# A selective-state scan on one core: projection tiles from a unit's first step, and D times xs by GpSimd in place of a weight product

## What is computed

```python
xz = h @ in_w
xs, z = jnp.split(xz, 2, axis=-1)          # 512 channels each
xs = jax.nn.silu(xs)
proj = xs @ xproj_w
dt = jax.nn.softplus(proj[..., :512] + dt_bias)
Bm, Cm = proj[..., 512:576], proj[..., 576:]   # 64 states
A = -jnp.exp(A_log)
def step(hst, ins):
    dt_t, B_t, C_t, x_t = ins
    dA = jnp.exp(dt_t[:, :, None] * A)
    hst = hst * dA + (dt_t * x_t)[:, :, None] * B_t[:, None, :]
    y_t = jnp.einsum('bds,bs->bd', hst, C_t)
    return (hst, y_t)
_, ys = jax.lax.scan(step, h0, (tm(dt), tm(Bm), tm(Cm), tm(xs)))
y = jnp.swapaxes(ys, 0, 1) + xs * Dskip
return y * jax.nn.silu(z) @ out_w
```

## The kernel before

| tile | what | pieces |
|---|---|---|
| xs (u+1), zs (u) | input projection, 4 tiles each | 2, each a 128x512 product of two passes (L1429) |
| bc (u+1) | B and C | 4 |
| dt (u+1) | dt, 4 tiles | 4 |
| out (u-1) | output projection, 2 tiles | 4 |
| yT (u-1), bT, dtxT (u+1) | four transposes (L1523, L1502, L1512) | 1 |

## Time and profile before

### The profile page before, as it was taken

One profiled execution on the slowest core, in us unless ns is written; L12 is line 12 of the kernel. 1 busy time (PEld: TensorE's weight loads), 2 busy tenths in 40 slices (PEclk: granted clock), 3 DMA queues, 4 the chain that ended last, 5 costly groups with the idle time before them and its releaser, 6 DMA issues.

```text
span 3270.9 us, 59384 instructions
## 1 busy us (share of the span) xinstructions
PE 3194.7 (98%) x22634; PEld 2505.6 (77%) x22634; DVE 2866.5 (88%) x2863; ACT 2815.5 (86%) x4659; POOL 2327.7 (71%) x1113
## 2 busy tenths in 40 slices
PE   8999999999999999999999999999999999999899
PEld 5888898999899998999998999999888542222244
DVE  3999999999999999999999999999999578888121
ACT  6999999999999999999999999999989436777620
POOL 1899999999999999999999999999878220000000
PEclk8999999999999999999999999999999999999999
DMA  3223222212222222222222222222212043422000
GB/s 121 69 84 81 80 72 69 72 67 72 69 73 93 70 70 75 72 69 72 73 73 74 67 72 67 74 68 71 86 57 69 29 102 59 77 34 31 15 7 20
DMA packets 199837, 218.82 MB, mean 67 GB/s; under 512 B 79969, under 2 KB 149601, under 8 KB 199297
## 3 DMA queue, kind: packets, MB, share of 16 engines
q1 hardware_dynamic: 199554, 215.02, 23.1%
HBM read 194.29 MB, written 18.19 MB: 65 GB/s over the span
## 4 chain that ended last, share of the span: by engine, by line
PE 76%; ACT 15%; DVE 6%; issue 3%; DMA 0%; POOL 0%; DVEq 0%; ACTq 0%; SPq 0%
PE psum L1661 21%; PE psum L1429 17%; PE psum L1655 16%; PE psum L1652 12%; ACT arena L1091 6%; ACT arena L1073 5%; PE psum L1739 4%; PE psum L1728 3%; DVE arena L1319 2%; PE psum L1712 2%; DVE row_max L1382 2%; PE psum L1681 1%; ACT arena L1116 1%; ACT arena L1076 0%; ACT arena L920 0%
## 5 line engine op out<-in xcount | busy, mean ns | idle before, releaser
L1319 DVE TENSOR_TENSOR_SCAN arena<-arena,psum 128x512 f32<-128x512 f32 x2048 | 2373.8, 1230 | 58.6 <-PE psum L1655 45.6
L789 POOL TENSOR_TENSOR arena<-arena 128x1024 f32<-128x1024 f32 x1024 | 2225.8, 2185 | 257.1 <-DVE arena L1319 233.5
L1091 ACT ACTIVATE arena<-arena,a_neg 128x512 f32<-128x512 f32 x2048 | 1442.9, 724 | 45.4 <-PE psum L1655 44.9
L1661 PE MATMUL psum<-ident,arena 128*128 128x128 f32 x8192 | 1231.9, 273 | 1.7 <-POOL arena L789 1.7
L1073 ACT ACTIVATE arena<-arena,bT 128x512 f32<-128x512 f32 x1536 | 1110.7, 723 | 0.0
L1655 PE MATMUL psum<-ident,arena 128*128 128x128 f32 x6144 | 1009.8, 273 | 0.0
L1661 PEld LDWEIGHTS psum<-ident,arena 128*128 128x128 f32 x8192 | 962.7, 141 | 2.1 <-POOL arena L789 2.1
L1652 PE MATMUL psum<-arena 128*128 128x128 f32 x4096 | 821.1, 282 | 31.8 <-ACT arena L1073 16.5
L1652 PEld LDWEIGHTS psum<-arena 128*128 128x128 f32 x4096 | 648.3, 191 | 246.6 <-issue 151.9
L1655 PEld LDWEIGHTS psum<-ident,arena 128*128 128x128 f32 x6144 | 744.2, 142 | 0.0
L1429 PE MATMUL psum<-arena 128*128 128x512 f32 (+1 forms) x1440 | 672.0, 587 | 5.2 <-DVE arena L1191 2.9
(11 more groups left out here) (118 smaller groups left out, 871.9 us busy)
## 6 DMA issues: line engine op xcount, KB each, us to landing
arena<-bc_dram SPq DMA_DIRECT2D x256, 512.0 KB, 3.7
arena<-diag_dram SPq DMA_DIRECT2D x224, 128.0 KB, 2.1
arena<-qk_dram SPq DMA_DIRECT2D x96, 128.0 KB
diag_dram<-arena SPq DMA_DIRECT2D x32, 256.0 KB, 4.4
qk_dram<-arena SPq DMA_DIRECT2D x8, 768.0 KB, 3.4
arena<-in_x SPq DMA_DIRECT2D x4, 512.0 KB, 10.5
arena<-skip_w SPq DMA_DIRECT2D x64, 32.0 KB, 2.0
arena<-sums_dram SPq DMA_DIRECT2D x64, 32.0 KB, 1.8
```

The lines of the kernel that those rows point to most:

```text
L789: pool.tensor_tensor(out[:, :, way], h_now[:, :, way], c_row, ALU.mult)\
L1091: act.activation(decay[:, w % AHEAD, f], dt_[:, u % 2, f], ACT.Exp, scale=a_neg[:, d, f, st:st + 1])\
L1319: dve.tensor_tensor_scan(hs[:, w % RING, f, rows][:, way], decay[:, w % AHEAD, f, way], psum[:, 4 + n % U_BANKS, way], end_state(w - DS, f ...
L1661: return pe.matmul(psum[:, c, f * P:(f + 1) * P], hs[:, w % RING, f, at:at + P], ident[:, :], is_transpose=True, start=False, stop=w % DS ...
```

## The change

Two parts. First, the table of pieces for units 1 to 6: the tiles of zs, xs and yT start in step 1 (in the order zs, xs, yT) where they started in step 4 (xs, yT, zs); bc, bT, silu and the first dt tile come three, two, three and three steps sooner; and each dt tile now takes five steps, four pieces and an empty one. Unit 0 keeps its table in constants of its own, unit 7 too.

Second, D times xs: `skip_w` and the eight ACT operations that made it go. POOL multiplies xs by D in place, 128x512 per block (`scale_skip`), in steps 48, 50, 60 and 62 for the next unit and four times before the first step for unit 0; each waits until that block's dt times xs is made and the last dt tile has read xs. PE adds the result to the sums by transposes, like the products with C (`turn_skip`): block 0 in `first_state`, behind the transposes of step 0, and blocks 1 to 3 at the head of PE's turns 3 to 5, four transposes each.

```diff
-SILU_STEP, LAST_SILU_STEP = 24, 18
+FIRST_SILU_STEP, SILU_STEP, LAST_SILU_STEP = 24, 21, 18
+SKIP_STEPS = (48, 50, 60, 62)
-BC_TURN, BT_TURN, DT_TURN, DTX_TURN, OUT_TURNS = 25, 29, 31, 52, (47, 60)
+BC_TURN, BT_TURN, DT_TURNS, DTX_TURN, OUT_TURNS = 22, 27, (28, 33, 38, 43), 52, (47, 60)
+FIRST_BC_TURN, FIRST_BT_TURN, FIRST_DT_TURNS = 25, 29, (31, 35, 39, 43)
...
-                place([step for k in range(NI) for step in (xs_[k], yT_[k], zs_[k])], 4)
-            at[BC_TURN] = ("bc", u + 1)
-            at[BT_TURN] = ("bT", u + 1)
+                place([step for k in range(NI) for step in (zs_[k], xs_[k], yT_[k])], 1)
+            at[BC_TURN if u else FIRST_BC_TURN] = ("bc", u + 1)
+            at[BT_TURN if u else FIRST_BT_TURN] = ("bT", u + 1)
             for f in range(NI):
-                at[DT_TURN + 4 * f] = ("dt", u + 1, f)
+                at[(DT_TURNS if u else FIRST_DT_TURNS)[f]] = ("dt", u + 1, f)
...
+            def scale_skip(u, f):
+                pool.tensor_scalar(xs[:, f], xs[:, f], d_skip[:, unit(u)[0], f:f + 1], 0.0, ALU.mult, ALU.add).then_inc(s["skip_ready"], 1)
...
+                    if st in SKIP_STEPS and u < UNITS - 1:
+                        f = SKIP_STEPS.index(st)
+                        pool.wait_ge(s["dtx_ready"], NI * (u + 1) + f + 1)
+                        pool.wait_ge(s["tile_full"], first["dt", u + 1, NI - 1] + 1)
+                        scale_skip(u + 1, f)
...
-                        act.activation(skip_w[:, d, f], ident[:, :], ACT.Copy, scale=d_skip[:, d, f:f + 1])\
-                           .then_inc(s["skip_w_ready"], 1)
...
+            def turn_skip(u, f, c):
+                if c == 0:
+                    pe.wait_ge(s["skip_ready"], NI * u + f + 1)
+                pe.matmul(psum[:, c, f * P:(f + 1) * P], xs[:, f, c * P:(c + 1) * P], ident[:, :],
+                          is_transpose=True, start=False, stop=False)
...
             def reduce_state(w, f):
+                st = w % DS
+                if f == 0 and st < NI:
+                    for c in range(TB):
+                        turn_skip(w // DS, st, c)
...
-                for f in range(NI):
-                    pe.matmul(psum[:, c, f * P:(f + 1) * P], xs[:, f, c * P:(c + 1) * P],
-                              skip_w[:, unit(u)[0], f], start=f == 0, stop=False)
                 for f in range(NI):
                     o = turn_h(w, f, c)
+                turn_skip(u, 0, c)
```

More of the change, by code:

```diff
@@ L160, in build @@
         bT = sb("bT", [P, 2, TB, DS])
-        skip_w = sb("skip_w", [P, 2, NI, P])
-        attn_sb = skip_w.rearrange("p a b c -> p a (b c)")
+        attn_sb = sb("attn_sb", [P, 2, HALF])
         ident = sb("ident", [P, P])
@@ L201, in build @@
             centred squared rstd_step rstd_ready normed h_ready
-            exp_step dt_ready dtx_ready skip_w_ready bc_rows_ready a_exp a_ready silu_ready
+            exp_step dt_ready dtx_ready skip_ready bc_rows_ready a_exp a_ready silu_ready
             dve_const uT_ready u_full decay_ready scan_done prod_done reduce_done gated
@@ L320, in act_turns @@
                     todo.append((kind,) + back[1:])
-            if st == (LAST_SILU_STEP if u == UNITS - 1 else SILU_STEP):
+            if st == (LAST_SILU_STEP if u == UNITS - 1 else SILU_STEP if u else FIRST_SILU_STEP):
                 todo.append(("silu", u + 1))
@@ L773, in make_dtx @@
                 pool.tensor_tensor(dtx[f % 2], dt_[:, u % 2, f], xs[:, f], ALU.mult).then_inc(s["dtx_ready"], 1)
+            def scale_skip(u, f):
+                pool.tensor_scalar(xs[:, f], xs[:, f], d_skip[:, unit(u)[0], f:f + 1], 0.0, ALU.mult, ALU.add).then_inc(s["skip_ready"], 1)
+            pool.wait_ge(s["ssm_small_in"], 80)
+            pool.wait_ge(s["tile_full"], first["bc", 0] + 1)
+            pool.wait_ge(s["dtx_ready"], NI)
+            for f in range(NI):
+                scale_skip(0, f)
             for u in range(UNITS):
@@ L942, in copy_yT @@
                    .then_inc(s["tile_free_act"], 1)
-            def skip_weights():
-                for d in range(2):
-                    for f in range(NI):
-                        act.activation(skip_w[:, d, f], ident[:, :], ACT.Copy, scale=d_skip[:, d, f:f + 1])\
-                           .then_inc(s["skip_w_ready"], 1)
             def do(order):
@@ L1661, in turn_h @@
                 return pe.matmul(psum[:, c, f * P:(f + 1) * P], hs[:, w % RING, f, at:at + P], ident[:, :],
-                                 is_transpose=True, start=False, stop=w % DS == DS - 1 and f == NI - 1)
+                                 is_transpose=True, start=w % DS == 0 and f == 0, stop=w % DS == DS - 1 and f == NI - 1)
+            def turn_skip(u, f, c):
[3 more added lines that the diff above has]
+                          is_transpose=True, start=False, stop=False)
             def reduce_state(w, f):
+                st = w % DS
+                if f == 0 and st < NI:
+                    for c in range(TB):
+                        turn_skip(w // DS, st, c)
                 if f % 2 == 0:
@@ L1677, in first_state @@
                 if c == 0:
-                    pe.wait_ge(s["skip_w_ready"], 2 * NI)
                     pe.wait_ge(s["prod_done"], 2 * (w + 1))
                 for f in range(NI):
-                    pe.matmul(psum[:, c, f * P:(f + 1) * P], xs[:, f, c * P:(c + 1) * P],
-                              skip_w[:, unit(u)[0], f], start=f == 0, stop=False)
-                for f in range(NI):
                     o = turn_h(w, f, c)
+                turn_skip(u, 0, c)
                 if c == TB - 1:
```

1 line of the change is left out of this document (removed).

## The result

The changed kernel takes 3286.38 us (median of 9 runs, 3282.46 to 3286.97) against 3274.95 us of the kernel before in runs beside it: ratio 1.0032, 95% interval 1.0022 to 1.0043. It is slower by 11.4 us, where 2.3 were predicted. That is inside the range, by 0.6 us, but the forecast "within 0.2%" is missed: it is 0.35%. The profiled execution took 3286.86 us, with a span of 3284.8. Of the runs further down, one execution of scale_only (4066.72 us, granted clock 0.75) and one of bT_sooner (12481.36 us, 0.554) were in a slow state and are left out of their medians.

What follows compares the result with a forecast made beforehand. Even units were taken as bound by PE's 4.81 us piece steps, odd mostly by DVE's 4.69; even +0.93, odd +0.4, unit 0 -1.7 sum to +2.3 us on 3275.02, giving 3277.3 us, range 3265 to 3287.

Steps and rivals of the forecast that it cites:

- two pieces now fall in turns 1 and 2, where the gatings hide them: -0.73: Even units, early turns: two pieces hidden under DVE's gatings, credited against the new transposes, -0.73 us a unit.
- the -1.47 of the three empty turns: Even units, dt tiles: three empty steps between piece steps each give back 0.49 us of PE's lead, -1.47 us.
- Behind bT there is no light step any more ... +0.19: Even units, behind bT: two light steps in a row become one and one with transposes, +0.19 us.
- 3.55 less 1.76, rounded down: -1.7: Unit 0, nothing gated: skip products of 3.55 us on PE's path become transposes of 1.76 us, -1.7 us.
- The skip transposes: PE's turns 3 to 5: transposes of D times xs are new PE work, +1.29 us even; +0.96 odd, lead counted.
- turn 2 is hidden: Units from 1 on: PE's work in turn 2 costs nothing, since DVE has four gatings of 0.6 us there.
- The late gating: PE's turn 1: a piece ahead of the last sums delays the first gating, +0.6 us even, +0.5 odd.
- Silu: Silus three steps sooner: ACT has one plain step less to gain lead, +0.45 us in units 1 to 6.
- runs of 10 scans: Sign that the forecast is right: even-unit DVE timeline shows runs of 10 scans behind each dt tile.
- the term of 0.2: GpSimd's new operations, taken as 1.0 us each: POOL's lag costs 0.2 us in an even unit, 0 odd.
- the rival built on this operation: GpSimd becomes the bound: operation slower than 1.2 us decides; 3280 us at 1.3, 3295 at 2; chance 0.12.
- the third rival: ACT takes the dt stretch: late evictions, bank not free, empty steps lost, +1.5 us a unit, 3286; chance 0.08.

Runs made afterwards that it cites:

- scale_only: Kernel before, with its old table of pieces, but D times xs by GpSimd and transposes as in the changed kernel; 3281.34 us, ratio 1.0019.
- bT_sooner: Changed kernel with bT in turn 26 in place of 27, so an empty turn stands between bT and the first dt tile; 3280.89 us.
- three_mended: Changed kernel with all D times xs transposes in turn 2, turn 1's piece behind slot 3, and silu, bc, dt, first out one step later; 3266.37 us, ratio 0.9974.
- scale_only_turn2: Kernel before with its old table, D times xs by GpSimd and all sixteen transposes in turn 2; 3272.08 us, ratio 0.9993.
- skip_turn2: Changed kernel with all sixteen transposes of D times xs in turn 2, none at the head of turns 3 to 5; 3278.52 us, ratio 1.001.
- piece_late: Changed kernel with the piece of turn 1 behind slot 3 in place of slot 1, so behind the last sums of the unit before; 3281.93 us.
- scale_twice: Changed kernel with a second GpSimd operation of the same size (times one) behind each D times xs, PE waiting for the second; 3289.09 us.
- table_only: Changed kernel's new table of pieces with the eight ACT operations and the old products by skip_w put back; 3283.86 us, ratio 1.0027.
- dt_no_gaps: Changed kernel with dt tiles in turns 31, 35, 39, 43 as before, empty turns 28 to 30 in a row; 3284.33 us.

## Why the prediction was right or wrong

The units: predicted +2.3, measured +7.8. In sum: even +0.93 predicted, +1.87 measured (mean of three); odd +0.4, +1.08; unit 0 -1.7, -0.3; unit 7 0, -0.8. That is 2.8 + 2.0 + 1.4 - 0.8 = 5.4 us missed. The terms of the prediction, sorted by the steps they act on, show where (difference to the kernel before, us):

| | steps 0-19 | 20-50 | 51-63 |
|---|---|---|---|
| even, predicted | +1.16 | -0.43 | +0.20 |
| unit 4, measured | +2.10 | -0.27 | 0.00 |
| odd, predicted | +1.46 | -1.05 | 0.00 |
| unit 5, measured | +1.74 | -0.79 | +0.01 |

In an even unit the miss stands in the first twenty steps. That steps 20 to 50 came out near the forecast is luck: errors of both signs cancel there, and without the wait for bT (bT_sooner) they make -1.19.

- **The even units: a gain that was counted twice.** The step that failed is "two pieces now fall in turns 1 and 2, where the gatings hide them: -0.73". The new table has as many pieces as the old one; three of them moved from steps 20 to 50 into steps 1 to 3. What a hidden piece saves is saved where it is missing, in steps 20 to 50, and that is already in the -1.47 of the three empty turns. In steps 0 to 19 three pieces are new, and hiding two of them leaves one to pay. three_mended, which has no late gating and no transposes in turns 3 to 5, takes 95.84 us for these steps, and scale_only_turn2, with the same D times xs and the old table, 95.45: +0.39, one piece step of 0.36, and not -0.73. Steps 6 to 19 show it: 66.4 to 66.5 us in every run with the new table, 66.04 or 66.05 in every run with the old one (unit 4).
- **The wait for bT, priced as a small loss of lead.** The second step that failed is "Behind bT there is no light step any more ... +0.19". I counted PE's work there and not the bank: bT and the first dt tile came closer by one turn, and ACT's eviction, no later than before, was no longer hidden. bT_sooner takes 0.93 us off steps 28 to 31 of an even unit. The same takes 0.4 of the 0.7 missed in an odd one.
- **Unit 0.** "3.55 less 1.76, rounded down: -1.7" took PE's work for PE's path. In turn 2 PE has 3.1 us less to do, and step 2 of the unit fell by 1.5 us only (7.71 to 6.18); the transposes in the next three turns cost 1.3 there, as priced. What took the rest is ACT's eviction, already there as a wait of 0.16 us before the piece. Gain 0.3, and 1.4 once all transposes stand in turn 2 and fill the wait (skip_turn2). These gains are rough: the same code of unit 0 took 324.1 to 324.6 us in seven profiles and 323.4 to 323.9 in three.
- **The skip transposes.** The steps came as said, 5.24 and 4.82 us for steps 4 and 5 of unit 4. Undoing them gives 1.18 to 1.2 us in an even unit (1.29 predicted) and 1.1 in an odd one (0.96 predicted). But that "turn 2 is hidden" and "PE keeps up" I took for granted whatever stands in it: with a piece added, 3.55 us of products are not hidden.
- **The late gating.** +0.6 and +0.5, measured 0.60 and 0.49 by piece_late. The row said 0.84 us; 0.7 to 0.8 was expected.
- **Silu.** +0.45 predicted. DVE's wait grew by 0.36 us in an even unit and by 0.17 in an odd one. One step later, with all that this edit moves, brings 0.4 in an odd unit and 0.1 in an even one (mean of three).
- **Empty turns.** Three of them were to be worth 1.47 less 0.4 for ACT in an even unit and 1.5 in an odd one, over none. Against three in a row they measured 0.6 and 1.2, with the wait for bT gone on both sides. If a bunch gives back one lead, 0.74 us in an even unit, that makes about 1.3 over none there, where 1.07 was predicted; this is an estimate, as no run has none. The size fits it; runs of 10 scans came nowhere as predicted, but 16, 8, 8.
- **GpSimd.** 1.0 us assumed, 0.73 measured in the scan, and no wait: the term of 0.2 was 0. The Trainium skill (GPSIMD Engine Reference, "Elementwise — side-by-side cycle accounting") has 769 ns for 512 elements of a tight loop; the trace agrees, with 0.73 (0.69 to 0.80), and the rival built on this operation, which decides from 1.2 us on, is out. At double length it does begin (scale_twice).
- **Unit 7** has an unchanged table and came out 0.8 us shorter. In other profiles it took 324.8 to 327.8 us; nothing here settles why.
- **The number.** Even units, in terms: the double count about +1.0, bT +0.7, silu -0.35, ACT and empty turns about -0.2, GpSimd -0.2; together the +0.94 missed. That 3286.38 lies in the range is luck. The range ends at 3287 because the third rival, evictions that come late, was priced at 3286. The bank of pieces is indeed not free in time, but at one place a unit, with ACT no later than before, and the empty turns keep their worth. And 3.6 us of the 11.4 do not lie in the scan at all.

**What stays open.** Beside the units, the profiled pair differ by 4.1 us in the start and 2.1 in the tail. The start is shown to vary. The tail has the same operations too, and in it a lower granted clock from 80 to 200 us behind the last scan, before and after:

```profile
2629.60:2669.60 40.00, 37.17 (x113) 19.02 (x113) 26.16 (x41) 12.60 (x20) 7.12 (x3) 0.96 0.38 79
2669.60:2709.60 40.00, 35.71 (x115) 15.69 (x113) 39.63 (x69) 12.08 (x25) 12.70 (x9) 0.92 0.44 111
2709.60:2749.60 40.00, 39.22 (x206) 11.14 (x206) 33.44 (x60) 28.05 (x55) 0.00 (x0) 0.95 0.09 12
```

```profile
2641.50:2681.50 40.00, 37.53 (x109) 18.93 (x108) 25.87 (x41) 12.07 (x19) 7.13 (x3) 0.91 0.42 79
2681.50:2721.50 40.00, 37.49 (x119) 16.27 (x117) 38.75 (x69) 12.63 (x25) 12.70 (x9) 0.91 0.41 107
2721.50:2761.50 40.00, 38.08 (x197) 10.96 (x201) 33.22 (x59) 27.43 (x54) 0.00 (x0) 0.92 0.11 16
```

It took 721.1 to 721.7 us in five of the fourteen profiles (table_only, dt_no_gaps and three_mended among them) and 722.8 to 723.5 in nine. It goes with that clock: in the stretch from 80 to 200 us behind the last scan the granted clock averages 0.94 in each of the five short tails, and 0.93 (three) or 0.91 (six) in the nine long ones. So the new code does not force a long tail. Whether it makes one likelier isn't shown; both profiles of the kernel before have the short one.

The medians are not free of such chance either. The nine executions of the changed kernel fall into groups, three at 3282.5 to 3282.8 us, one at 3284.2 and five at 3286.4 to 3287.0, while those of the kernel before spread from 3272.4 to 3276.7. The fastest of each differ by 10.1 us, the medians by 11.4, where the units make 7.8. Most other variants lie 1.5 to 4.5 us over their units too (skip_turn2: +4.2 and -0.2), and two lie 0.3 and 0.7 under (scale_only_turn2, dt_no_gaps). So 2 to 4 us of the 11.4 are shown not to lie in the scan, and are not explained beyond this.

## What to carry to other kernels

Before a piece is moved closer to another in a shared buffer, look up who empties the buffer and when: the empty turn behind bT had hidden an eviction that then cost 0.93 us a unit, and a wait of 0.16 us in a row grew to 1.74 as soon as the work ahead of it got shorter. When work is moved, count it once where it leaves and once where it arrives: a piece hidden behind a stall saves its time only at the place that it left. The room behind a stall (here four gatings) is a budget in microseconds; it hides 1.76 us of transposes and a piece, and not 3.55 us of products and a piece. A step that frees PE and a table that uses the freed time are to be tried together, and single edits beside them: three of them, each worth 1.2 to 2.4 us for an even and an odd unit together, turned 11 us of loss into 9 of gain.
